# Reordered splits, gathers and routing in a two-stage mixture-of-experts kernel

## The chip, the core and the metric

One core of a Trainium2 chip runs the whole program. The metric is the device time of one execution in microseconds; lower is better. The engines are TensorE (PE, matmul), VectorE (DVE), ScalarE (ACT), GpSimd (POOL) and SyncE (SP), each with its own queue of instructions, which wait on semaphores; DMA queues move data beside them.

## The reference, cut to what matters

The network has four sublayers; attention and a first mixture of experts come before the ones that matter here and are left out below. `x` has 2 x 1024 tokens of 256 numbers.

```python
# _L1_cond: 8 routed experts (top 2) and 2 shared ones, all computed for every token
gp = _leaky(jnp.einsum('th,ehm->etm', x, w_gate))      # hidden width 128
up = jnp.einsum('th,ehm->etm', x, w_up)
y_all = jnp.einsum('etm,emh->eth', gp * up, w_down)
y = (y_sel * topk_w[..., None]).sum(1) + p              # p: the two shared experts
# _L1_ffn, on that y: 8 experts, top 2 by a softmax router
probs = jax.nn.softmax(xf @ w_router, axis=-1)
topk_w, topk_idx = jax.lax.top_k(probs, 2)
h = jax.nn.gelu(jnp.einsum('te,ieh->tih', xf, w1) + b1) # hidden width 1024
out = jnp.einsum('tih,ihe->tie', h, w2) + b2
out = jnp.sum(out * weights[..., None], axis=1)         # weights: zero for experts not chosen
x = x + out
```

## The kernel before

Two stages are touched. All matmuls use float32r in three products: each operand is split into a rounded high part (a copy, mostly on ScalarE) and a low part (a subtraction, on VectorE or POOL), and high x low, low x high and high x high are summed in PSUM.

**The dense stage** (lines 1380 to 1873; 400 to 596 us of the profile from its first steps on) computes `_L1_cond` as 40 steps `s`. A step is one expert and one chunk of 512 tokens. The first eight steps belong to the shared experts. Then the routed experts come, with two chunks each: first for half 0 of the tokens (16 steps, up to `FIRST_HALF` = 24), then for half 1. A group `g` is the steps that share an expert's weights. TensorE runs `up(s + 2)` (L1611, into `pU` and `pG`) and then `down(s)` (L1622, into `pY`). Between them, for one step, ScalarE copies `pG` (L1711), VectorE makes the leaky product (L1786, L1791), ScalarE makes `hidh` (L1731), POOL makes `hidl` (L1551), and VectorE adds `pY` into `xc` (L1851). The expert's next weights are split into `gparts` and `dparts` by ScalarE's `keep_up`, `keep_down` (L1687, L1690) and POOL's `rest_up`, `rest_down` (L1495, L1499), written out in the same per-step loops. `keep_up(g)` waits until `up` of group g - 2 is done. Each engine executes in order, so what is written ahead of `hidh` or `hidl` is in front of them in the queue.

While half 1 is computed, half 0 is routed by pieces of `Slots(0, ...)`, written into the same loops: top 2 (`dve_first`, `dve_second`), `act_exp`, counts, blocks, places, `pool_tokens`, `pe_find`, `dve_tables`. They end in tables `gidx` and `sidx` (tokens of each block of 288). The rows with their probabilities are stored to `ytab` by `sp_rows` (L1284). Near the end, POOL issues `gather(0)`.

**The second phase** (lines 1876 to 2102, from 596 us) computes `_L1_ffn` by blocks of 288 gathered tokens. There are 16 visits `q`, one per half and expert, half 0 first; with these inputs each visit has one block, `j` = `q`. For one block, TensorE does fc1 in 8 chunks `c` of 6 matmuls each (L2001 to L2003, into `pH` with three banks), in the middle `turn_back(j)` (L1975, the block before, transposed into `pX`), after fc1 `turn(j + 1)` (L1364, the next block's rows, into the same `pX`), then fc2 (48 matmuls, L2014 to L2016). ScalarE does 8 gelus (L2042), `gated` in their middle (L2034, scales the turned output by the token's probability `gk` into `yg`), `columns_high` (L1369, `xh`; L1371, `gk`), both high parts of the next expert's weights (L2026, L2027, `keep_high`) and the output's bias (L2055, `yT`). VectorE splits `h` (L2081, L2083), `xl` (L1375) and the weights' low parts (L2068, L2072). POOL's body is `scatter(j)` (L1941, three indirect DMAs that add `yg` to the result) and then `gather(j + 2)` (L1358, three indirect DMAs from `ytab` into `G`). `gather(j + 2)` needs `turn(j + 1)`, which reads the one buffer `G`; `gated(j + 1)` needs `scatter(j)` to have landed, for `yg` is one buffer too. SP loads the weights of split `r`, two DMAs of 1 MB, into a ring of four, as soon as the low parts of split r - 4 are made.

In visits 0 to 5, half 1 is routed by `Slots(1, ...)` on a bank of its own (`pF`). Half 1's rows go to `ytab` from SP's queue, behind the load of r = 3.

## Time and profile before

| | us |
|---|---|
| median of 3 runs | 885.27 |
| lowest, highest | 878.69, 886.39 |
| the profiled execution | 884.36 |
| its span | 882.5 |
| TensorE busy (matmul) | 694.8 (79%) |
| VectorE busy | 474.9 (54%) |
| POOL busy | 395.0 (45%) |
| ScalarE busy | 336.0 (38%) |

The profile is one execution; its span runs from the first to the last recorded instruction. Times in it count from the span's start. A row of the timeline has the start, the duration of all instructions merged in it, the engine, the line of the kernel, the operation with out <- in and the number of instructions, and, in brackets, how long the engine had stood idle in front of it and what released it. "Granted clock" (PEclk) is TensorE's clock as a share of 2.4 GHz; it is granted at two levels, 1.2 and 2.4 GHz, and a share between them is a mean over a stretch. TensorE's matmul records overlap, so its busy time is an upper bound of useful work.

### The profile page before, as it was taken

How to read it: one execution, taken by the hardware profiler on the slowest of the kernel's cores; microseconds unless marked ns; L12 is line 12 of the kernel's file. 1: busy time of each engine (PE TensorE's matmuls, PEld its weight loads, DVE VectorE, ACT ScalarE, POOL GpSimd, SP SyncE). 2: the span in 40 equal slices, each digit the busy share in tenths (PEclk: the TensorE clock that was granted, in tenths of full speed). 3: DMA queues.
4: the chain of work that ended last, by engine and by line, in shares of the span. 5: the costliest groups of instructions: out<-in, count | busy, mean ns of one | idle time of the engine just before them, and what ended most of it. 6: DMA issues, size and time to landing. Idle time of an engine off the chain costs nothing. (4 is left out here: it accounts for less than half of the span.)

```text
span 882.5 us, 14235 instructions
## 1 busy us (share of the span) xinstructions
PE 694.8 (79%) x4385; PEld 636.3 (72%) x4386; DVE 474.9 (54%) x1023; ACT 336.0 (38%) x739; POOL 395.0 (45%) x515
## 2 busy tenths in 40 slices
PE   0777777511699999399989989978888989898991
PEld 0676667501699889387778867768778989898991
DVE  3353554478311111256877788866647855565760
ACT  1243445110133323124233332316746556475660
POOL 2222202000145445423554657636747665755873
PEclk9756675655799999769999999999999989898996
DMA  7870490040089994594000102006496463562222
GB/s 236 136 182 14 108 325 0 6 117 4 13 273 320 299 308 121 161 321 148 25 24 25 36 25 74 1 15 212 129 354 148 119 188 82 138 206 46 42 45 31
DMA packets 91760, 111.56 MB, mean 126 GB/s; under 512 B 9632, under 2 KB 80672, under 8 KB 91296
## 3 DMA queue, kind: packets, MB, share of 16 engines
q1 hardware_dynamic: 75072, 90.74, 33.4%
q0 software_dynamic: 11536, 14.30, 9.5%
q10 hardware_dynamic: 5072, 5.52, 1.9%
q8 instruction: 42, 0.69, 0.3%
q14 instruction: 38, 0.31, 0.1%
HBM read 93.84 MB, written 17.32 MB: 126 GB/s over the span
## 5 line engine op out<-in xcount | busy, mean ns | idle before, releaser
L1941 POOL DMA_INDIRECT out<-nyg,si x51 | 88.6, 1737 | 20.5 <-issue 20.2
L121 POOL TENSOR_TENSOR held<-ones 128x1 f32<-128x1 f32 x137 | 45.8, 334 | 116.2 <-ACT nyg L2034 53.8
L2042 ACT ACTIVATE nh<-npH,c_sb 128x288 f32<-128x288 f32 x128 | 62.1, 502 | 39.1 <-PE npH L2003 36.9
L1358 POOL DMA_INDIRECT nG<-ytab,gi x54 | 63.9, 1184 | 14.6 <-issue 13.0
L2081 DVE CAST nhh<-nh 128x576 fp32r<-128x576 f32 x64 | 33.0, 516 | 66.6 <-ACT nh L2042 66.6
L1851 DVE SCALAR_TENSOR_TENSOR xc<-pY,W,xc 128x264 f32<-128x264 f32 x160 | 67.3, 483 | 2.7 <-PE pY L1622 2.7
L1551 POOL TENSOR_TENSOR hidl<-sums,hidh 128x512 fp32r<-128x512 f32 x40 | 56.1, 1403 | 23.5 <-ACT hidh L1731 23.5
L1611 PE MATMUL pU<-xparts,gparts 128*128 128x512 f32 x240 | 65.5, 409 | 1.1 <-DVE xparts L1782 1.1
L1611 PE MATMUL pG<-xparts,gparts 128*128 128x512 f32 x240 | 64.1, 403 | 2.5 <-ACT sums L1711 2.5
L1786 DVE SCALAR_TENSOR_TENSOR sums<-sums 128x512 f32<-128x512 f32 x40 | 40.9, 1023 | 42.2 <-ACT sums L1711 41.7
L1104 PEld LDWEIGHTS mpH<-mXT,w_sb 128*128 128x128 f32 x512 | 61.2, 196 | 1.8 <-DVE mXT L1135 1.1
L1104 PE MATMUL mpH<-mXT,w_sb 128*128 128x128 f32 x512 | 61.5, 280 | 0.7 <-DVE mXT L1135 0.7
L1622 PE MATMUL pY<-dparts,hidh 128*128 128x264 f32 x320 | 60.7, 284 | 0.0
L1622 PE MATMUL pY<-dparts,hidl 128*128 128x264 f32 x160 | 47.7, 298 | 14.8 <-POOL hidl L1551 8.2
L1123 ACT ACTIVATE mhT<-mpH,b_sb 128x128 f32<-128x128 f32 x128 | 36.1, 371 | 59.6 <-PE mpH L1104 59.6
L1112 PE MATMUL mpY<-w_sb,mhT 128*128 128x256 f32 x256 | 58.2, 380 | 0.0
L1611 PEld LDWEIGHTS pG<-xparts,gparts 128*128 128x128 f32 x240 | 46.3, 194 | 14.3 <-ACT sums L1711 3.2
L1112 PEld LDWEIGHTS mpY<-w_sb,mhT 128*128 128x128 f32 x256 | 47.4, 190 | 6.0
L1611 PEld LDWEIGHTS pU<-xparts,gparts 128*128 128x128 f32 x240 | 44.0, 195 | 9.4 <-DVE xparts L1782 1.5
L1622 PEld LDWEIGHTS pY<-dparts,hidh 128*128 128x128 f32 x320 | 49.7, 188 | 0.8
L2083 DVE TENSOR_TENSOR nhl<-nh,nhh 128x576 fp32r<-128x576 f32 x64 | 48.6, 759 | 2.2
L1495 POOL TENSOR_TENSOR gparts<-gw,gparts 128x512 fp32r<-128x512 f32 x18 | 23.4, 1298 | 58.8 <-ACT gparts L1687 48.1
(412 smaller groups left out, 1891.8 us busy)
## 6 DMA issues: line engine op xcount, KB each, us to landing
w_sb<-in_w SPq DMA_DIRECT2D x32, 1024.0 KB, 8.3
w_sb<-in_v SPq DMA_DIRECT2D x30, 1024.0 KB, 9.8
bias_sb<-in_bias SPq DMA_DIRECT2D x4, 1024.0 KB, 14.2
gw<-in_wgate SPq DMA_DIRECT2D x17, 128.0 KB, 2.2
gw<-in_wup SPq DMA_DIRECT2D x17, 128.0 KB, 2.3
ytab<-xc SPq DMA_DIRECT2D x2, 1056.0 KB, 5.1
acc<-zrow SPq DMA_DIRECT2D x1, 2056.0 KB, 24.6
sums<-acc SPq DMA_DIRECT2D x4, 514.0 KB, 6.0
```

The costliest lines, as they stand in the source:

```text
L121: pool.tensor_tensor(held[:, n:n + 1], ones[:, 0:1], ones[:, 0:1], ALU.mult)
L1104: ins = pe.matmul(pH[:, c // 4, (c % 4) * P:(c % 4 + 1) * P], w1_sb[:, u, k, c * P:(c + 1) * P], XT[:, k], start=(k == 0), stop=(k == KD - 1))
L1112: ins = pe.matmul(pY[:, 0:D], hT[:, c], w2_sb[:, u, c], start=(c == 0), stop=(c == FC - 1))
L1358: pool.indirect_dma_start(G[:, n], None, ytab, bass.IndirectOffsetOnAxis(ap=gi3[:, n:n + 1], axis=0)).then_inc(gathered, 16)
L1551: pool.tensor_tensor(hidl[:, s % 2], hid[:, s % 2], hidh[:, s % 2], ALU.subtract).then_inc(lo_ready, 1)
L1611: ins = pe.matmul(pp, gparts[:, g % 2, wn, cs], xparts[:, xn, k, chunk], start=(k == 0 and (wn, xn) == (0, 1)), stop=(k == KD - 1 and (wn, ...
L1622: ins = pe.matmul(pY[:, j, 0:YROW], hn[:, s % 2, j * P:(j + 1) * P], dparts[:, e, wn], start=(hn is hidl), stop=(hn is hidh and wn == 0))
L1786: dve.scalar_tensor_tensor(lk, ga, 0.01, ga, ALU.mult, ALU.max).then_inc(lk_ready, 1)
L1851: dve.scalar_tensor_tensor(xc[:, t], pY[:, j, 0:YROW], W[:, t, e:e + 1], xc[:, t], ALU.mult, ALU.add).then_inc(acc_done, 1)
L1941: pool.indirect_dma_start(result, bass.IndirectOffsetOnAxis(ap=si3[:, n:n + 1], axis=0), yg[:, n], None, bounds_check=B * N - 1, oob_is_er ...
L2042: act.activation(h[:, c], pH[:, c % HBANKS, 0:WIDE], ACT.Gelu_apprx_tanh, bias=c1_sb[:, e, c:c + 1]).then_inc(gelu_done, 1)
L2083: dve.tensor_tensor(hl[:, two], h[:, two], hh[:, two], ALU.subtract).then_inc(h_ready, 1)
```

## The change

- Dense stage: ScalarE and POOL make `hidh` and `hidl` at the start of their part of a step, and the splits, constants and token products stand behind them. `keep_up` and `rest_up` of group g are placed in step first_of[g] - 3 instead of first_of[g] - 4. The last routing pieces of half 0 come one step earlier, and `gather(0)` is placed in the last step, behind its `hidl`, instead of the last but one.
- Second phase: POOL gathers first and scatters second. `turn_back` gets two banks `pZ` of its own, stands behind fc1 next to `turn`, and `gated` stands behind `columns_high` and the first weight split. `pH` has two banks instead of three, and half 1's routing pieces use a part of `pZ`. `gk` has four slots instead of two.
- Half 1's routing: the matmul pieces follow the first chunk of fc1 in visits 1, 2, 3 and 6, and TensorE waits ahead of `turn_back` until they are read. VectorE's pieces stand at a visit's start. `pool_tokens` go to visits 4 and 5, ahead of the gather. The exponential and the counts stand ahead of visit 1's gelus. ScalarE stores half 1's rows in visit 2.

```diff
@@ -1197 @@
-        gk = sb("gk", [SUB, 2 * NSUB, E1], into=late)
+        gk = sb("gk", [SUB, 4 * NSUB, E1], into=late)
@@ -1216 @@
-        M_SET, LESS, PROBS, BLOCKS = range(1, 5)
+        M_SET, LESS, PROBS, BLOCKS, READ = range(1, 6)
@@ -1235, class Slots @@
                 self.pC = bank[0:TE, TE:TE + P]
-                self.pT = bank[0:E1, TE + P:TE + 2 * P]
-                self.pN = bank[0:1, TE + 2 * P:TE + 2 * P + E1]
-                self.pM = bank[0:SUB, TE + 2 * P + E1:TE + 2 * P + E1 + self.cols]
+                self.pT = bank[0:E1, TE:TE + P]
+                self.pM = bank[0:SUB, TE:TE + self.cols]
+                self.pN = bank[0:1, TE + P:TE + P + E1]
...
-            def sp_rows(self, sp):
+            def rows_out(self, eng):
...
-                link(dve.tensor_copy(nblk[:, self.hf], self.pN))
+                dve.tensor_copy(nblk[:, self.hf], self.pN).then_inc(r_dve, 1)
@@ -1532, dense stage, POOL @@
                     for s in range(LAST + 1):
                         e, c = STEPS[s]
+                        pool.wait_ge(hi_ready, s + 1)
+                        if s >= 2:
+                            pool.wait_ge(down_done, 4 * s - 4)
+                        pool.tensor_tensor(hidl[:, s % 2], hid[:, s % 2], hidh[:, s % 2], ALU.subtract).then_inc(lo_ready, 1)
                         if s == 1:
                             rest_up(1)
                         for g in range(2, len(GROUPS)):
-                            if first_of[g] - 4 == s:
+                            if first_of[g] - 3 == s:
                                 rest_up(g)
...
+                        if s == FIRST_HALF + 8:
+                            slots.pool_tokens(pool, 0)
                         if s == FIRST_HALF + 9:
-                            slots.pool_tokens(pool, 0)
-                        if s == FIRST_HALF + 10:
                             slots.pool_tokens(pool, 1)
-                        pool.wait_ge(hi_ready, s + 1)
-                        if s >= 2:
-                            pool.wait_ge(down_done, 4 * s - 4)
-                        pool.tensor_tensor(hidl[:, s % 2], hid[:, s % 2], hidh[:, s % 2], ALU.subtract).then_inc(lo_ready, 1)
...
-                        if s == LAST - 1:
+                        if s == LAST:
                             pool.wait_ge(tables, 1)
                             pool.wait_ge(y_out, 16)
                             gather(pool, 0, 0)
@@ -1668, dense stage, TensorE @@
-                        if s == FIRST_HALF + 11:
+                        if s == FIRST_HALF + 10:
                             slots.pe_find(pe)
@@ -1720, dense stage, ScalarE @@
-                        for g in range(2, len(GROUPS)):
-                            if first_of[g] - 4 == s:
-                                keep_up(g)
-                        if s == 2 or 6 <= s < FIRST_HALF - 2 and s % 2 == 0:
-                            keep_down(1 if s == 2 else GROUPS[group_at[s + 2]])
                         act.wait_ge(hid_ready, s + 1)
                         if s >= 2:
                             act.wait_ge(down_done, 4 * s - 4)
                         act.activation(hidh[:, s % 2], hid[:, s % 2], ACT.Copy).then_inc(hi_ready, 1)
+                        for g in range(2, len(GROUPS)):
+                            if first_of[g] - 3 == s:
+                                keep_up(g)
+                        if s == 2 or 6 <= s < FIRST_HALF - 2 and s % 2 == 0:
+                            keep_down(1 if s == 2 else GROUPS[group_at[s + 2]])
@@ -1866, dense stage, VectorE @@
-                        if part == 12:
+                        if part == 11:
                             slots.dve_tables(dve, slot_link)
@@ -1885, second phase @@
-            pH = ps("npH", [P, 3, 512], ph)
+            pZ = ps("npZ", [P, 2, 512], ph)
+            pH = ps("npH", [P, 2, 512], ph)
             pY = ps("npY", [P, 2, 512], ph)
-            pF = ps("npF", [P, 512], ph)
-            slots = Slots(1, pF, A1, hot1, tok1s)
-            HBANKS = 3
+            slots = Slots(1, pZ[:, 1, D:2 * D], A1, hot1, tok1s)
+            HBANKS = 2
@@ -1923, SP @@
-                        if r == RING - 1:
-                            slots.sp_rows(sp)
@@ -1948, POOL @@
+                        if first and q in (4, 5):
+                            slots.pool_tokens(pool, q - 4)
...
-                        scatter(j, hf)
                         pool.wait_ge(turned, j + 2)
                         pool.wait_ge(gk_ready, j + 2)
                         pool.wait_ge(gathered, j * (16 * NSUB) + 32 * NSUB)
                         held_here(pool, 1)
                         gather(pool, j + 2, hf)
-                        if first and q == 4:
-                            for n in range(2):
-                                slots.pool_tokens(pool, n)
+                        scatter(j, hf)
@@ -1969, TensorE @@
-                                ins = pe.transpose(pX[0:SUB, n // 2, (n % 2) * D + k * P:(n % 2) * D + (k + 1) * P],
+                                ins = pe.transpose(pZ[0:SUB, n // 2, (n % 2) * D + k * P:(n % 2) * D + (k + 1) * P],
...
+                        if first and q in (1, 2, 3, 6):
+                            pe.wait_ge(yg_ready, j)
                         for c in range(FC):
-                            if c == FC // 2:
-                                turn_back(j)
-                                if first and q == 1:
-                                    slots.pe_count(pe)
...
                             ins.then_inc(fc1_done, 1)
-                        pe.wait_ge(yg_ready, j + 1)
+                            if first and c == 0:
+                                if q == 1:
+                                    slots.pe_count(pe)
...
+                                if q == 6:
+                                    slots.pe_find(pe)
+                        if first and q == 1:
+                            pe.wait_ge(r_act, 2 + COPIED)
+                        if first and q in (2, 3):
+                            pe.wait_ge(r_dve, 5 + (BLOCKS if q == 2 else READ))
+                        if first and q == 6:
+                            pe.wait_ge(tables, 2)
+                        turn_back(j)
                         turn(pe, pX, j + 1)
@@ -2024, ScalarE @@
-                    def keep_high(r):
+                    def first_high(r):
                         act.wait_ge(w_in[r % RING], 32 * (W_ROUND + 1 + r // RING))
                         act.activation(w1h[r % 2], raw1[r % RING], ACT.Copy).then_inc(w_hi, 1)
+
+                    def second_high(r):
                         act.activation(w2h[r % 2], raw2[r % RING], ACT.Copy).then_inc(w_hi, 1)
                     def gated(j, e):
-                        slot = (j + 1) % 2
+                        slot = (j + 3) % 4
...
+                        if first and q == 1:
+                            slots.act_exp(act)
+                            slots.act_counts(act)
                         for c in range(FC):
                             act.wait_ge(fc1_done, j * FC + c + 1)
                             act.activation(h[:, c], pH[:, c % HBANKS, 0:WIDE], ACT.Gelu_apprx_tanh,
                                            bias=c1_sb[:, e, c:c + 1]).then_inc(gelu_done, 1)
-                            if c == FC // 2:
-                                gated(j, VISITS[max(q - 1, 0)][1] if first else e)
                         columns_high(act, pX, j + 1)
-                        if first and q == 1:
-                            slots.act_exp(act)
-                            slots.act_counts(act)
-                        if first and q + 1 < 2 * E1 and split_of[q + 1] != split_of[q]:
+                        split = first and q + 1 < 2 * E1 and split_of[q + 1] != split_of[q]
+                        if split:
                             act.wait_ge(fc2_done, j + 1)
-                            keep_high(split_of[q + 1])
+                            first_high(split_of[q + 1])
+                        gated(j, VISITS[max(q - 1, 0)][1] if first else e)
+                        if split:
+                            second_high(split_of[q + 1])
+                        if first and q == 2:
+                            slots.rows_out(act)
@@ -2075, VectorE @@
                     def body(j, q, first):
+                        if first and q == 0:
+                            slots.dve_second(dve, slot_link)
+                        if first and q == 1:
+                            slots.dve_probs(dve, slot_link)
+                        if first and q == 2:
+                            slots.dve_blocks(dve, slot_link)
+                        if first and q == 3:
+                            slots.dve_places(dve, slot_link)
+                        if first and q == 6:
+                            slots.dve_tables(dve, slot_link)
                         for p in range(FC // 2):
...
-                        if first and q == 5:
-                            slots.dve_tables(dve, slot_link)
```

## Rows read from the trace of the kernel before

**Rows 1.** Busy time by stretch: a quiet block, then one with a stall; start:end, length, engines, PEclk.

```profile
724.00:738.00 14.00, 14.00 (x111) 13.99 (x110) 5.57 (x9) 6.40 (x15) 6.00 (x9) 1.00 0.66 180
...
752.00:772.00 20.00, 17.03 (x112) 16.79 (x111) 11.02 (x12) 10.06 (x17) 15.38 (x20) 0.83 0.60 152
```

**Rows 2.** TensorE's waits from 596 us on: us in total, times, longest.

```profile
PE npX L1364 <- DMA nG<-ytab,gi: 18.9, 6, 5.0
```

**Rows 3.** TensorE's waits from 400 to 596 us, same columns.

```profile
PE pY L1622 <- POOL hidl L1551: 8.2, 10, 2.9
```

**Rows 4.** Timeline, TensorE: starts of four `up` steps; start, duration, then [idle before <- releaser].

```profile
427.31 1.55 PE L1611 MATMUL pU<-xparts,gparts 128*128 128x512 f32 x6
...
503.55 0.63 PE L1611 MATMUL pU<-xparts,gparts 128*128 128x512 f32 x2
...
507.79 1.55 PE L1611 MATMUL pU<-xparts,gparts 128*128 128x512 f32 x6
...
581.50 1.56 PE L1611 MATMUL pU<-xparts,gparts 128*128 128x512 f32 x6
```

**Rows 5.** Timeline, ScalarE, one of the dense stage's splits (`keep_up`).

```profile
465.70 0.63 ACT L1687 ACTIVATE gparts<-gw 128x512 fp32r<-128x512 f32 x1 [4.03 <-PE pG L1611]
```

**Rows 6.** Timeline: ScalarE releases TensorE, in the routing part of the dense stage.

```profile
526.22 0.58 ACT L1711 ACTIVATE sums<-pG 128x512 f32<-128x512 f32 x1
...
526.86 1.42 PE L1611 MATMUL pG<-xparts,gparts 128*128 128x512 f32 x5 [2.48 <-ACT sums L1711]
```

**Rows 7.** Timeline, end of the dense stage and start of the second phase.

```profile
585.38 0.58 POOL L1354 COPY gi<-gidx 96x3 uint32<-96x3 uint32 x1 [1.05 <-DVE sidx L1350]
...
586.67 0.63 ACT L1731 ACTIVATE hidh<-sums 128x512 fp32r<-128x512 f32 x1 [1.58 <-DVE sums L1791]
...
590.48 1.31 POOL L1551 TENSOR_TENSOR hidl<-sums,hidh 128x512 fp32r<-128x512 f32 x1
...
594.79 0.76 DVE L1375 TENSOR_TENSOR nxl<-pU,nxh 128x576 fp32r<-128x576 f32 x1 [0.58 <-ACT nxh L1369]
...
597.65 0.60 PE L2001 MATMUL npH<-nxh,w1l 128*128 128x288 f32 x1 [3.58 <-issue]
```

**Rows 8.** Timeline, ScalarE, a quiet block: gelus, then a weight split.

```profile
835.22 1.01 ACT L2042 ACTIVATE nh<-npH,c_sb 128x288 f32<-128x288 f32 x2 [0.19 <-issue]
836.52 0.50 ACT L2042 ACTIVATE nh<-npH,c_sb 128x288 f32<-128x288 f32 x1 [0.29 <-PE npH L2003]
...
842.30 1.90 ACT L2026 ACTIVATE w1h<-w_sb 128x2048 fp32r<-128x2048 f32 x1
```

**Rows 9.** Timeline: gather, scatter, a stalled turn, and the next gather beside VectorE's splits.

```profile
755.99 1.14 POOL L1358 DMA_INDIRECT nG<-ytab,gi  x1 [0.30 <-issue]
...
758.47 0.19 POOL L121 TENSOR_TENSOR held<-ones 128x1 f32<-128x1 f32 x1 [1.00 <-ACT nyg L2034]
...
762.12 1.22 PE L1364 MATMUL npX<-ident,nG 96*128 96x96 f32 x6 [2.97 <-DMA nG<-ytab,gi]
...
762.97 1.43 POOL L1941 DMA_INDIRECT out<-nyg,si  x1 [0.30 <-issue]
...
765.97 2.29 DVE L2068 TENSOR_TENSOR xparts<-w_sb,xparts 128x2048 fp32r<-128x2048 f32 x1 [1.15 <-ACT xparts L2026]
...
769.37 1.87 POOL L1358 DMA_INDIRECT nG<-ytab,gi  x1 [0.30 <-issue]
```

**Rows 10.** Timeline, ScalarE: one of two table loads around half 1's exponential.

```profile
622.79 1.28 ACT L1269 ACT_TABLE_LOAD   x1
```

**Rows 11.** Timeline, the kernel's tail.

```profile
862.58 0.89 ACT L2055 ACTIVATE nyT<-npY,c_sb 128x288 f32<-128x288 f32 x2 [5.64 <-PE npY L2016]
864.72 1.19 ACT L2034 ACTIVATE nyg<-npX,gk 96x256 f32<-96x256 f32 x3 [1.25 <-PE npX L1975]
...
873.67 0.19 POOL L121 TENSOR_TENSOR held<-ones 128x1 f32<-128x1 f32 x1 [1.95 <-DMA out<-nyg,si]
```

**Rows 12.** DMA issues from 596 us on: last number is median us from issue to landing.

```profile
out<-nyg,si POOLq DMA_INDIRECT x51, 3.6
```

More of the change, by code:

```diff
@@ L1279, in dve_probs @@
                 dve.tensor_tensor(router_rows(self.hf), hexp[:], bcast(hred[:, 3], E1), ALU.mult).then_inc(r_dve, 1)
-            def sp_rows(self, sp):
-                sp.wait_ge(r_dve, 4 * self.hf + PROBS)
+            def rows_out(self, eng):
+                eng.wait_ge(r_dve, 5 * self.hf + PROBS)
                 rows = slice(self.hf * HT * P, (self.hf + 1) * HT * P)
-                sp.dma_start(ytab[rows, :].rearrange("(t p) d -> p t d", p=P),
+                eng.dma_start(ytab[rows, :].rearrange("(t p) d -> p t d", p=P),
                              xc[:, self.hf * HT:(self.hf + 1) * HT]).then_inc(y_out, 16)
@@ L1369, in columns_high @@
             act.activation(xh[:], pX[:, :, 0:WIDE], ACT.Copy).then_inc(xh_ready, 1)
-            slot = ds((j % 2) * NSUB, NSUB) if not isinstance(j, int) else slice((j % 2) * NSUB, (j % 2 + 1) * NSUB)
+            slot = ds((j % 4) * NSUB, NSUB) if not isinstance(j, int) else slice((j % 4) * NSUB, (j % 4 + 1) * NSUB)
             act.activation(gk[:, slot], G[:, :, D:YROW], ACT.Copy).then_inc(gk_ready, 1)
@@ L1986, in body @@
                         pe.wait_ge(x_ready, j + 1)
+                        if first and q in (1, 2, 3, 6):
+                            pe.wait_ge(yg_ready, j)
                         for c in range(FC):
-                            if c == FC // 2:
-                                turn_back(j)
-                                if first and q == 1:
-                                    slots.pe_count(pe)
-                                if first and q == 2:
-                                    slots.pe_totals(pe)
-                                if first and q == 3:
-                                    slots.pe_places(pe)
-                                if first and q == 5:
-                                    slots.pe_find(pe)
                             pe.wait_ge(gelu_done, j * FC + c + 1 + FC - HBANKS if c >= HBANKS else j * FC + FC)
@@ L2087, in body @@
                             low_second(split_of[q + 1])
-                        if first and q == 0:
-                            slots.dve_second(dve, slot_link)
-                        if first and q == 1:
-                            slots.dve_probs(dve, slot_link)
-                        if first and q == 2:
-                            slots.dve_blocks(dve, slot_link)
                         if first and q == 3:
-                            slots.dve_places(dve, slot_link)
                             slots.dve_hot(dve, 0)
@@ L2098, in body @@
                             slots.dve_hot(dve, 1)
-                        if first and q == 5:
-                            slots.dve_tables(dve, slot_link)
                     per_block(dve, "dve", body)
```

16 lines of the change are left out of this document (10 added, 6 removed).

## The prediction

> **What bounds the kernel now.** I read the busy table of single stretches first, then TensorE's waits, then the timeline at the places that these name. TensorE sets the pace of both stages that the diff touches. In a quiet block of the second phase it is busy for the whole 14.0 us at full clock; in another block of the same work the stretch is 20 us long, TensorE is busy for 17.0 of it, and the granted clock is 0.83 [rows 1]. The difference is the turn of the next block's rows, which waits for gathered data: 18.9 us in 6 waits, the longest 5.0 [rows 2]. A stall costs more than its length. A wait of 2.97 [rows 9] makes that block 6.0 longer, because the matmuls behind it run at 1.2 GHz for a while. The sixteen blocks take 264.9 us, from the first matmul at 597.65 [rows 7] to the end of the last fc2 at 862.5 [rows 11], where sixteen quiet ones would take 224.
>
> In the dense stage, TensorE waits 8.2 us in 10 waits for `hidl` on POOL [rows 3]. A free step is 4.24 us long (503.55 to 507.79). The 17 steps from 427.31 to 507.79 take 80.5 instead of 72.1, so 8.4 are lost; the 14 from 507.79 to 581.50 take 73.7 instead of 59.4, so 14.3 are lost [rows 4]. In the first of these stretches the reader sees why: ScalarE stands idle 4.03 us in front of `keep_up`, waiting for TensorE's later `up` [rows 5], and `hidh` of the step, ready long before, is queued behind it; `hidl` comes later still.
>
> The sum is made against the profiled execution: 884.4 us with a span of 882.5. The median of the three runs is 885.3, 0.9 above it.
>
> **Part 1, dense order.** `hidh` and `hidl` now go first, and the splits follow one step later (first_of - 3), by when the `up` that they wait for is done: the 4.03 wait vanishes. The split is still due only when TensorE reaches that group, about two steps (8.5 us) after it can start, which covers one ScalarE and one POOL instruction of 0.6 and 1.3 us (`hidl` has 1.31 in [rows 7]). POOL's constants and token products also go behind `hidl`. Of the 8.4 I take 7. Of the 14.3, VectorE's routing chain is the cause of at least the 2.48 wait [rows 6] and routing matmuls are real work; neither goes away, and I take 5. Sum: 12 us gained. Bounds: 4, if little more than the listed waits other than the last goes, and 16.
>
> **Part 2, first gather.** `gather(0)` moves behind the last `hidl`. Before, it starts at 585.38 and holds that `hidl` until 590.48 [rows 7], which is the longest wait of [rows 3] (2.9). In the new order the last `hidl` can start when its `hidh` ends, 587.3, and end at 588.6; the gather follows. With 5.1 for its copy and its issues, the third of these starts about 1.5 before their end, at 592.2; landing takes between 3.6 [rows 12] and 6.1 (755.99 to the turn at 762.12 [rows 9]). Turn, `xh` and `xl` add 2.2, so x is ready at 598.0 to 600.5, where it was 595.55 [rows 7]. I take the quiet landing, since no weight load runs there: 2.5 us lost (bounds 2.5 and 5). The routing pieces of half 0 move one step forward, so the tables are not late.
>
> **Part 3, gather ahead of scatter.** Times here count from the end of a turn. In the block behind the stall at 762.12 (the turn ends at 763.34) the gather waited for nothing but this turn: its third issue ended at 771.24, 7.9 after it, with VectorE's weight splits alongside [rows 9]. In the new order every gather runs like this one. Its third issue starts at 6.0 and lands between 9.6 and 12.1; the next turn starts at about 13.5. So the data come 1.4 to 3.9 early and the six stalls go. A second cause goes with them: the router rows left SP's queue, where they held back the loads of r = 4 to 6 until half 1's probabilities were ready. Now ScalarE issues that store, one instruction, in a place with idle time. In exchange the loads of r = 2, 3 and 4 all start with the phase, and `gather(1)` lands among them. I put 1 us on this.
>
> **Part 4, two banks instead of three for fc1.** In a quiet block ScalarE makes a gelu in 0.50 and idles 0.29 per chunk [rows 8]. With two banks this 0.29 is the whole slack for the handoff and for TensorE's drain. A matmul starts 0.06 after the ScalarE instruction that releases it (526.80 to 526.86 [rows 6]), so the steady chunks just fit. The first chunk of a block does not: its gelu starts at 835.22, after the bias of the block before and a gap of 0.19 [rows 8], about 0.3 later than the data. I take 0.4 per block, 6.4 in all (bounds 0 and 12). TensorE's turn into banks of its own is as long as before, and only moves.
>
> **Part 5, half 1's routing.** At q = 1 the exponential and the counts now stand ahead of the first gelu: two table loads of 1.28 [rows 10] and two short copies, 3.1 us, of which 0.3 is hidden: 2.8, and 1.2 for a fall of the clock that may follow (0 to 3.0, the price in [rows 1] and [rows 9]). The counting, totals, places and find matmuls stay the same work, 4.9.
>
> **Part 6, the scatter's buffer and the tail.** Behind a gather come the scatters. From 757.13 to 764.40 they took 7.3, of which 1.0 was a wait for ScalarE [rows 9]; so the third now starts at 7.9 + 4.85 = 12.75, POOL is free at 14.2, and at 3.6 [rows 12] it lands at 16.4. Next block's `gated`, which overwrites `yg`, wants this landing at its own turn + 2.6, that is 14.4 + 2.6 = 17.0, and ScalarE has 0.5 to spare behind it (one split is 1.90 [rows 8]). It fits by about 1 us; under a weight load, with 6.1, it doesn't. I put 2 us on it. At the end nothing covers it. Before, the last `gated` starts at 864.72 and the scatter behind it has landed at 873.67 [rows 11]. Now it waits for the preceding scatter to land. Without splits beside its gather (2.3 less) that is 16.4 - 2.3 = 14.1 after the turn, or, with 6.3 for fc2, 7.8 after the last fc2, where `gated` started 2.2 after it. The tail grows by 5.6 us.
>
> **The sum.** Second phase: 224 + 6.4 + 2.5 (cold start, as now) + 4.0 + 4.9 = 241.8 against 264.9, 23.1 gained. In all: -12 + 2.5 - 23.1 + 1 + 2 + 5.6 = -24.0, so 884.4 - 24 = 860.
>
> **A rule against it.** SBUF — State Buffer (the Trainium skill), section "SBUF: two separate sides", says that some VectorE instructions hold the port pair that POOL shares for their whole length, and that POOL writes no descriptors meanwhile. Parts of the trace agree: an issue beside the splits took 1.87, where one of another gather without them took 1.14 [rows 9]. By the rule a gather that meets two splits would be stopped for all of both.
>
> **The rivals.** *POOL is held for both splits in full:* one split is 2.29 [rows 9], two are 4.6, and the 7.9 holds about half of that already. POOL would then be free at 16.5 instead of 14.2. The next gather can begin 0.8 after its turn, so a block would last 15.7 instead of 14.4; thirteen blocks with splits make 860 + 17 = 877. Against it: the 7.9 was measured beside two splits. Chance 0.08.
> *The dense gain turns into waits for VectorE*, which has its own chain there [rows 6]: 3 instead of 12, 869. Chance 0.10.
> *The gathers still come late*, the change not doing what it says: landing would have to take over 7.5. At three of six stalls with 6.0 each: 878. The longest landing in [rows 9] is 6.1, against it. Chance 0.06.
> *Slower than before:* POOL becomes the bound. The place is POOL's queue, gather and then scatter in each block, with `gated` behind the landing. It decides against the kernel when a block takes 16.7 instead of 14.4, that is from a POOL free at 17.5, 3.3 later than the rows give; fifteen blocks then cost 34.5, 894.5. Against it stands that all the pieces are measured; for it, that the slack is only 1 us and that the splits, scatter and loads meet in a new order. Chance 0.07.
> *Better:* two banks cost nothing, the dense stage gains 16, and the clock holds: 860 - 6.4 - 4 - 1.2 = 848. Chance 0.14.
>
> **The numbers.** The forecast has 0.52, with a range of its own of 852 to 868; the remaining 0.03 lies between the cases. About 1% (8.9 us) is what a measurement of this kernel tells from no change, so faster means below 876.4. The forecast, the better case, the dense rival and some of the remainder give 0.81; the two cases at 877 and 878 fall within 1% and give, with a little of the remainder, 0.12; slower is 0.07. The range of 846 to 877 takes in the forecast, the dense rival and most of the better case, and leaves out about 0.2.
>
> **What would show it.** In the changed kernel's waits, TensorE's turn should have at most one wait for `nG`, and blocks of the second phase should be 14.3 to 14.7 apart at granted clock 1.0. ScalarE's `keep_up` should lose its wait for TensorE, and the dense steps should be 4.24 to 4.3 outside the routing chain. The last `gated` should start about 7.8 after the last fc2. A wait of TensorE for gelu in every chunk would show part 4 wrong; POOL busy from turn to turn without a pause, or `gated` waiting for a scatter, part 6. The forecast is wrong most easily in part 6, where 1 us of slack per block decides.

## The result, and the profile after

The kernel after takes 856.1 us (median; 855.4 to 857.8) where the kernel before takes 882.0 on the same chips: 0.970 of it, with an interval of 0.966 to 0.974. Forecast were 860.0, in a range of 846 to 877. The profiled execution has a span of 853.6 against 882.5.

That span is 28.9 shorter, but not all of it is the change's. I cut both spans at three points: the start of the dense stage's fourth `up` step, which comes 13.6 us behind the third (router matmuls stand between them); the first fc1 matmul; the last bias of fc2. What follows the last bias is the tail. A block is counted from bias to bias.

| us | ahead of the dense steps | dense steps to first fc1 | sixteen blocks | tail | span |
|---|---|---|---|---|---|
| before | 406.1 | 191.6 | 264.9 | 19.9 | 882.5 |
| after | 401.8 | 182.6 | 244.0 | 25.2 | 853.6 |
| difference | -4.3 | -9.0 | -20.9 | +5.3 | -28.9 |

The first column is code that the change leaves alone, but for the first three dense steps. In the fourteen profiles of this case it ends anywhere from 397.2 to 411.7 (402.8 in d2 below, which has the dense stage of before), so its -4.3 is not counted as the change's. The change itself is worth the other three, -24.6; the medians say -25.9.

The blocks, as busy time by stretch of the kernel after (start:end, length, then TensorE, weight loads, VectorE, ScalarE, GpSimd, granted clock, DMA share, GB/s): the first block, half 1's exponential (q = 1), two blocks beside weight splits with a quiet one between:

```profile
584.35:601.11 16.76, 16.72 (x108) 16.43 (x108) 10.56 (x20) 9.65 (x17) 6.11 (x8) 0.84 1.04 364
601.11:618.36 17.25, 15.18 (x112) 14.57 (x113) 10.87 (x15) 13.22 (x21) 11.46 (x13) 1.00 0.56 173
650.07:665.95 15.88, 14.64 (x110) 14.04 (x108) 13.66 (x13) 10.12 (x19) 13.36 (x13) 1.00 0.61 175
712.02:726.23 14.21, 14.21 (x110) 14.00 (x109) 8.85 (x11) 10.35 (x18) 8.64 (x9) 1.00 0.24 35
755.96:771.79 15.83, 15.60 (x118) 15.08 (x116) 10.12 (x11) 10.28 (x19) 13.32 (x16) 1.00 0.60 177
```

Against [rows 1] none of the sixteen blocks is 20 us long and only the first has a granted clock under 1.0. Quiet blocks are those without weight splits or routing. TensorE's waits from 400 us on (total, times, longest):

```profile
PE npH L1990 <- ACT nh L2051: 5.6, 6, 1.6
...
PE pU L1364 <- DMA nG<-ytab,gi: 4.0, 1, 4.0
...
PE pY L1622 <- POOL hidl L1538: 0.2, 1, 0.2
```

The six waits for `nG` of [rows 2] are gone; one is left, at the first turn. `hidl` fell from 8.2 [rows 3] to 0.2. New are six waits for a gelu. The dense stage in the timeline: the three `up` steps that answer to the first, third and fourth of [rows 4], and one `keep_up` for [rows 5]:

```profile
422.99 1.32 PE L1611 MATMUL pU<-xparts,gparts 128*128 128x512 f32 x5
...
496.27 1.55 PE L1611 MATMUL pU<-xparts,gparts 128*128 128x512 f32 x6
...
566.62 1.56 PE L1611 MATMUL pU<-xparts,gparts 128*128 128x512 f32 x6
...
459.95 0.62 ACT L1687 ACTIVATE gparts<-gw 128x512 fp32r<-128x512 f32 x1
```

Seventeen steps now take 73.3 (80.5), the next fourteen 70.4 (73.7), and `keep_up` waits for nothing. The end of the stage, for [rows 7]:

```profile
572.38 1.29 POOL L1538 TENSOR_TENSOR hidl<-sums,hidh 128x512 fp32r<-128x512 f32 x1 [2.85 <-ACT hidh L1726]
573.61 0.18 POOL L1354 COPY gi<-gidx 96x3 uint32<-96x3 uint32 x1
...
579.57 1.19 PE L1364 MATMUL pU<-ident,nG 96*128 96x96 f32 x6 [4.04 <-DMA nG<-ytab,gi]
581.48 0.76 DVE L1375 TENSOR_TENSOR nxl<-pU,nxh 128x576 fp32r<-128x576 f32 x1 [5.04 <-ACT nxh L1369]
584.35 0.60 PE L1990 MATMUL npH<-nxh,w1l 128*128 128x288 f32 x1 [3.58 <-issue]
```

From the last `up` to the first fc1 it is 17.73, where it was 16.15. The end of one of the long blocks, ScalarE's waits for a scatter from 584 to 830 us, and the landing of the scatters (issue lines, last number), for [rows 12]:

```profile
768.90 1.19 ACT L2040 ACTIVATE nyg<-npZ,gk 96x256 f32<-96x256 f32 x3 [2.56 <-DMA out<-nyg,si]
769.98 1.91 ACT L2033 ACTIVATE w2h<-w_sb 128x2048 fp32r<-128x2048 f32 x1
771.79 0.88 ACT L2065 ACTIVATE nyT<-npY,c_sb 128x288 f32<-128x288 f32 x2
...
773.11 0.40 PE L1990 MATMUL npH<-nxh,xparts 128*128 128x288 f32 x1 [1.39 <-ACT nh L2051]
...
ACT nyg L2040 <- DMA out<-nyg,si: 20.9, 11, 3.4
...
out<-nyg,si POOLq DMA_INDIRECT x51, 5.0
```

The gates (`gated`) wait 2.56 for the scatter; behind them stand the second weight split and the bias; the gelus are late and TensorE stops 1.39. The median landing went from 3.6 to 5.0, and this is a mixture. Blocks 0 to 11, in which weights are loaded, and the rest, in which none are:

```profile
out<-nyg,si POOLq DMA_INDIRECT x33, 5.9
...
out<-nyg,si POOLq DMA_INDIRECT x18, 3.4
```

In before the same two are 3.8 and 3.5. The tail, for [rows 11]:

```profile
828.39 0.89 ACT L2065 ACTIVATE nyT<-npY,c_sb 128x288 f32<-128x288 f32 x2 [1.02 <-PE npY L2020]
835.99 1.19 ACT L2040 ACTIVATE nyg<-npZ,gk 96x256 f32<-96x256 f32 x3 [6.71 <-DMA out<-nyg,si]
...
844.79 0.19 POOL L121 TENSOR_TENSOR held<-ones 128x1 f32<-128x1 f32 x1 [1.89 <-DMA out<-nyg,si]
```

### The profile page after: what moved, and what is told of

It reads as the page before. It is cut to its first block and busy times, and to the rows that moved or that the text cites. A ratio compares the mean times of both kernels' runs of the same rounds, so it can differ in the third digit from the quotient of the medians.

```text
span 853.6 us, 14267 instructions
## 1 busy us (share of the span) xinstructions
PE 681.3 (80%) x4385; PEld 624.7 (73%) x4386; DVE 477.6 (56%) x1023; ACT 341.7 (40%) x739; POOL 401.6 (47%) x515
## 5 line engine op out<-in xcount | busy, mean ns | idle before, releaser
L1939 POOL DMA_INDIRECT out<-nyg,si x51 | 82.2, 1611 | 17.9 <-issue 17.9
L1538 POOL TENSOR_TENSOR hidl<-sums,hidh 128x512 fp32r<-128x512 f32 x40 | 52.2, 1305 | 76.4 <-ACT hidh L1726 76.4
L1358 POOL DMA_INDIRECT nG<-ytab,gi x54 | 77.4, 1434 | 16.3 <-issue 16.2
L1726 ACT ACTIVATE hidh<-sums 128x512 fp32r<-128x512 f32 x40 | 25.3, 631 | 80.3 <-DVE sums L1791 80.3
L1786 DVE SCALAR_TENSOR_TENSOR sums<-sums 128x512 f32<-128x512 f32 x40 | 38.8, 970 | 28.7 <-ACT sums L1711 28.1
L2103 DVE TENSOR_TENSOR nhl<-nh,nhh 128x576 fp32r<-128x576 f32 x64 | 50.9, 796 | 2.2
L2101 DVE CAST nhh<-nh 128x576 fp32r<-128x576 f32 x64 | 31.8, 497 | 30.9 <-ACT nh L2051 30.6
```

Source lines behind the costliest of these rows:

```text
L1358: pool.indirect_dma_start(G[:, n], None, ytab, bass.IndirectOffsetOnAxis(ap=gi3[:, n:n + 1], axis=0)).then_inc(gathered, 16)
L1538: pool.tensor_tensor(hidl[:, s % 2], hid[:, s % 2], hidh[:, s % 2], ALU.subtract).then_inc(lo_ready, 1)
L1786: dve.scalar_tensor_tensor(lk, ga, 0.01, ga, ALU.mult, ALU.max).then_inc(lk_ready, 1)
L1939: pool.indirect_dma_start(result, bass.IndirectOffsetOnAxis(ap=si3[:, n:n + 1], axis=0), yg[:, n], None, bounds_check=B * N - 1, oob_is_er ...
L2103: dve.tensor_tensor(hl[:, two], h[:, two], hh[:, two], ALU.subtract).then_inc(h_ready, 1)
```

## Experiments

The columns are those of the table above, from each kernel's profiled execution; the ratio is to the kernel before, timed beside it.

| kernel | median us | ratio, interval | dense to fc1 | blocks | tail |
|---|---|---|---|---|---|
| d1, dense part alone | 872.7 | 0.992 [0.988, 0.995] | 182.1 | 260.3 | 19.9 |
| d2, second phase alone | 867.9 | 0.986 [0.980, 0.992] | 194.0 | 244.3 | 25.2 |
| d3, order without late splits | 858.6 | 0.976 [0.969, 0.982] | 187.5 | 243.8 | 25.3 |
| d4, late splits without order | 858.1 | 0.979 [0.969, 0.989] | 185.5 | 243.7 | 25.2 |
| p1, scatter first | 913.0 | 1.035 [1.029, 1.040] | 181.8 | 303.7 | 20.9 |
| c1, gather first, old banks | 937.8 | 1.064 [1.058, 1.069] | 182.3 | 324.6 | 24.0 |
| p2, two `yg` | 855.7 | 0.970 [0.965, 0.975] | 182.6 | 248.4 | 24.6 |
| p6, second split ahead of gates | 855.5 | 0.970 [0.965, 0.975] | 182.1 | 244.9 | 25.2 |
| p4, first gather early | 855.1 | 0.969 [0.964, 0.975] | 179.6 | 243.7 | 25.2 |
| b1, five edits | 861.7 | 0.976 [0.970, 0.982] | 183.8 | 245.4 | 24.7 |
| b2, b1 with another tail | 859.4 | 0.976 [0.970, 0.981] | 182.9 | 247.9 | 23.8 |
| b3, tokens on VectorE | 850.3 | 0.966 [0.962, 0.971] | 182.7 | 241.2 | 21.3 |

### The two parts, each alone (d1, d2)

d1 takes only the dense hunks into the kernel before, d2 takes them out of the kernel after. In d1, for instance:

```diff
-                            if first_of[g] - 4 == s:
+                            if first_of[g] - 3 == s:
...
-                        if s == LAST - 1:
+                        if s == LAST:
```

> The kernel before with the change's dense hunks alone (hidden block's high and low parts ahead of the weight splits, splits three steps ahead, half 0's tokens and tables one step earlier, first gather behind the last low part); second phase as before. Theory (the two parts add up): the dense part ends 14.9 us earlier and the first turn loses 1.6 us of it, as the two traces put up(39) and the first fc1 matmul, so about 13.3 us under the kernel before: 867 to 870 where before is 882. Rival (the gain of the dense part depends on the second phase, or the second phase's late gathers swallow it): 875 to 882.

> The kernel after with its dense hunks undone (dense part as before, second phase as after). Theory: the sixteen blocks keep their 20.9 us and the tail its loss of 5.2 us, so about 15.7 us under the kernel before: 865 to 868 where before is 882. Rival (the second phase gains because the dense part left something ready for it): 872 to 880.

d2 came as expected. d1 fell between the two cases, and the expectation was at fault: its 14.9 compared two clock times, and 4.3 of them belong to the stage ahead. By its own stage d1 gains 9.5, about what after does (9.0). Its ten executions lie between 863.0 and 875.5, and the profiled one is the fastest; those of after lie within 2.4. By medians d1 gains 7.9 and d2 12.8, and these fall 5 short of the 25.9 of both. Of this, 2.4 is visible: d2, which has the dense stage of before, takes 194.0 there instead of 191.6, with a granted clock of 0.76 from the last `up` to the first fc1, where before has 1.00. The rest is not explained. What d1 also gives is a bound for the price of two banks: it has three, and its quiet blocks, in the same view as above, are 13.9 long, against 14.2 in after. Of the 0.3, fc1 has 0.2 and the moved `turn_back` 0.1; no run changes the banks alone.

```profile
784.99:798.89 13.90, 13.90 (x110) 13.89 (x109) 9.39 (x11) 10.12 (x18) 6.70 (x7) 1.00 0.18 25
```

### Order or lateness of the splits (d3, d4)

d3 sets the distance back to four steps; d4 moves the high and low parts back behind the splits.

```diff
-                            if first_of[g] - 3 == s:
+                            if first_of[g] - 4 == s:
```

> The kernel after, with the splits of the next expert's weights back at four steps ahead; the hidden block's high and low parts stay ahead of them. Theory (what cost the dense part was the split's WAIT standing ahead of the high part, so that order alone gives most): at most 3 us over the kernel after, 856 to 859. Rival (the wait costs wherever it stands, since the next step's high part is behind it): 8 us or more over it, 864 to 868.

> The kernel after, with the high and low parts of the hidden block back behind the weight splits; the splits stay three steps ahead, where their wait for TensorE's previous use of the buffer is over. Theory (the wait was the cost, so its lateness alone gives most too): at most 4 us over the kernel after, 856 to 860. Rival (the splits' own time ahead of the high and low part is the cost, some 1 us on ScalarE and 2 to 4 us on GpSimd in every second step): 8 us or more over it, 864 to 870.

Both medians are where the theory put them, 2.5 and 2.0 over after, too near each other to rank (d4's four executions are 856.3 to 859.0 and one of 869.1). The stage itself tells more. From the fourth to the last `up` it takes 175.4 before, 170.3 in d3, 168.1 in d4 and 164.8 in after. The starts of the `up` steps that answer to the first, third and fourth of [rows 4], d3 and then d4:

```profile
423.69 1.55 PE L1611 MATMUL pU<-xparts,gparts 128*128 128x512 f32 x6
...
497.49 1.56 PE L1611 MATMUL pU<-xparts,gparts 128*128 128x512 f32 x6
...
571.22 1.56 PE L1611 MATMUL pU<-xparts,gparts 128*128 128x512 f32 x6
```
```profile
422.17 1.55 PE L1611 MATMUL pU<-xparts,gparts 128*128 128x512 f32 x6
...
495.05 1.55 PE L1611 MATMUL pU<-xparts,gparts 128*128 128x512 f32 x6
...
569.10 1.56 PE L1611 MATMUL pU<-xparts,gparts 128*128 128x512 f32 x6
```

The seventeen steps take 73.8 and 72.9 (before 80.5, after 73.3): there either half of the edit is enough by itself. In d3 `keep_up` still waits, some 1.2 at a time, and does no harm behind `hidh`; in d4 it does not wait, and the splits' own time ahead of `hidl` costs nothing. So what cost these steps was the wait standing ahead of `hidh`. One `keep_up` of d3:

```profile
458.06 0.63 ACT L1687 ACTIVATE gparts<-gw 128x512 fp32r<-128x512 f32 x1 [1.23 <-PE pG L1611]
```

The fourteen steps with the routing take 73.7 and 74.1, as before (73.7), and 70.4 in after: there neither half alone gains anything. In d4 two waits for `hidl` make 4.6; the longer one stands behind a token product, for which GpSimd had waited 7.11 ahead of `hidl`:

```profile
541.64 2.16 POOL L1328 TENSOR_TENSOR w_sb<-w_sb,token 128x432 f32<-128x432 f32 x1 [7.11 <-DVE w_sb L1321]
...
545.07 0.59 PE L1622 MATMUL pY<-dparts,hidl 128*128 128x264 f32 x1 [3.54 <-POOL hidl L1551]
```

In d3 the loss is spread over several waits, with a granted clock of 0.98, and its cause stays open.

### Gather first, and the banks that it needs (p1, c1)

p1 turns the two calls in GpSimd's body round again. c1 is d1 with the same two calls in the new order, and nothing else of the second phase.

```diff
-                        scatter(j, hf)
                         pool.wait_ge(turned, j + 2)
...
                         gather(pool, j + 2, hf)
+                        scatter(j, hf)
```

> The kernel after with GpSimd's body turned round again: scatter of the block before first, then the gather; banks, four gate slots and everything else as after. Theory (part 3: the order is what ended the six stalls): gates at 2.1 us after a quiet turn, scatter issues to 7.6, gather issues to 11.8, landing 2.8: data at 14.6 after a turn, for a next turn due at 13.4, so 1 us late in quiet blocks and 3 to 5 in those with weight splits: 20 to 45 us over the kernel after, 876 to 900, with waits for the gathered rows in most blocks. Rival (the gathers have slack in either order; the gain came from the turns' own banks): within 4 us of the kernel after, 854 to 860.

> The kernel before with the dense part of after and one more line: GpSimd issues the gather before the scatter; three banks for fc1, the turn and the turn back in one bank pair, gates in the middle of fc1 as before. Theory (gathering first needs the turns' own banks: the gates wait for the scatter, which lands some 15 us after a turn's end, and the next turn waits for the gates, which were due 3 us ahead of it): no wait for gathered rows, but a wait for the gates of 2 to 5 us at nearly every turn, 890 to 915, slower than the 873 of the dense part alone. Rival (the order alone ends the six stalls and the banks are not needed): 854 to 862.

TensorE's waits, p1 and then c1:

```profile
PE npX L1364 <- DMA nG<-ytab,gi: 44.1, 13, 4.9
```
```profile
PE npX L1364 <- ACT nyg L2034: 49.0, 12, 7.0
```

Both went the theory's way and further: the expectations left out the clock behind each wait (granted clocks down to 0.83 over a block of p1 and 0.77 in c1), and c1 waits another 7.4, once, for half 1's token product. p1 shows that in the new arrangement the order ends the late gathers. It has the router rows off SP's queue as after has, so that alone does not end them. c1 shows that in the old arrangement the order only trades them for the gates, which must empty the bank that the turn wants and wait for the scatter now standing behind the gather. Either half alone is slower than before.

### The long blocks (p2, p6)

p2 gives the gates two buffers in turn; p6 moves one line, shown here.

```diff
                             first_high(split_of[q + 1])
+                            second_high(split_of[q + 1])
                         gated(j, VISITS[max(q - 1, 0)][1] if first else e)
-                        if split:
-                            second_high(split_of[q + 1])
```

> The kernel after with two buffers for the gated rows, so that the gates of a block no longer wait for the landing of the scatter just issued (they wait for the one before). Theory (the blocks of 15.2 to 16.2 us under weight splits are long because the gates wait for the scatter, the second weight split, the bias and the first gelu stand behind them): blocks 2 to 4, 10 and 11 come to about 14.6, 5 to 6 us in all, 850 to 852. Rival (they are long because VectorE's low parts of the weights stand ahead of the hidden low parts): no change, 855 to 857.

> The kernel after with one line moved: in a block with a weight split ScalarE makes the high part of the second matrix right behind that of the first, and the gates come behind both. Theory (as for the two buffers: the second split is late because the gates wait for the scatter): 3 to 6 us under the kernel after, 850 to 853, and the gates 1.9 us later at no cost. Rival (the gates' lateness then delays the bias and the scatter as much): 855 to 858.

The totals did not move, so as a forecast both fell. The blocks did: 2, 4 and 11, which were 15.6, 15.9 and 15.8 long, became 14.8, 14.3, 14.5 in p2 and 14.6, 14.2, 14.5 in p6. The gain went elsewhere: in both at block 5, from 14.4 to 20.4 and 21.0, and in p2 at block 3 as well, from 16.2 to 18.5, behind a wait of 1.27 ahead of the routing matmuls (granted clock 0.91). Block 5 in p2's timeline:

```profile
657.57 3.04 DVE L2078 TENSOR_TENSOR xparts<-w_sb,xparts 128x2048 fp32r<-128x2048 f32 x1 [1.15 <-ACT xparts L2030]
657.91 2.73 POOL L121 TENSOR_TENSOR held<-ones 128x1 f32<-128x1 f32 x1
658.04 4.79 POOL L1354 COPY gi<-gidx 96x3 uint32 x1
660.53 2.28 DVE L2082 TENSOR_TENSOR w2l<-w_sb,w2h 128x2048 fp32r<-128x2048 f32 x1
...
673.07 0.71 PE L1364 MATMUL npX<-ident,nG 96*128 96x96 f32 x6 [4.45 <-DMA nG<-ytab,gi]
```

With the second split no longer held up, VectorE runs both without a gap, and half 1's tokens (2.01) had kept GpSimd back until then. Its two short instructions, `held` of 128x1 and the list copy of 96x3, take 0.19 and 0.18 where nothing stands beside them. Here the first ends with the first split and the copy with the second, and TensorE waited 4.45 for the gather behind them. In after the same two splits stood 2.1 us apart and GpSimd's list had been copied ahead of both (the first starts at 661.72):

```profile
659.17 0.18 POOL L1354 COPY gi<-gidx 96x3 uint32 x1
```

A missing gap alone is not the cause. In before and in p6 VectorE runs all fourteen pairs of splits without one, and GpSimd loses a whole pair at one place in each: where the list copy meets it. A gather whose list is copied already gets its issues in, each some 1.3 longer. The trace of before has both cases:

```profile
626.38 4.49 POOL L1354 COPY gi<-gidx 96x3 uint32 x1
...
766.80 2.27 POOL L1358 DMA_INDIRECT nG<-ytab,gi  x1 [0.30 <-issue]
```

The clock added to the price. In p6 the corresponding wait is 3.83, and block 5 is 6.6 longer than in after; over the ten microseconds behind the wait the granted clock was 0.69.

```profile
672.50:682.40 9.90, 9.90 (x56) 9.90 (x57) 5.27 (x3) 5.48 (x8) 9.05 (x8) 0.69 0.20 25
```

### The first gather (p4)

```diff
-                        if s == LAST:
+                        if s == LAST - 1:
                             pool.wait_ge(tables, 1)
```

> The kernel after with the first gather one step earlier, where before had it (behind the low part of the last step but one, ahead of that of the last). Theory (part 2: its issues hold GpSimd for 3.5 us, which the low part of the last step must wait for): the last step's down matmuls wait 2 to 4 us, the first turn does not wait; the first fc1 comes within 1 us of that of after, 855 to 858. Rival (there is room for it): 2.5 to 4 us under the kernel after, 852 to 854.

The end of the dense stage in p4's timeline:

```profile
572.65 1.30 POOL L1538 TENSOR_TENSOR hidl<-sums,hidh 128x512 fp32r<-128x512 f32 x1
...
574.00 0.39 PE L1622 MATMUL pY<-dparts,hidl 128*128 128x264 f32 x1 [1.66 <-POOL hidl L1538]
...
579.81 0.60 PE L1990 MATMUL npH<-nxh,w1l 128*128 128x288 f32 x1 [3.58 <-issue]
```

The trace sides with the rival: TensorE waits only 1.66 for the last low part, and the first fc1 comes 14.8 after the last `up`. It takes 17.2 to 17.8 in after, d1, d3, d4, p1, p2 and p6, which all have the late gather, so by the traces the change's move of this gather costs 2.4 to 3.0. The median is 1.0 under after's, with executions from 850.5 to 857.3, and cannot settle it.

### Together (b1, b2, b3)

b1 takes p2, p6 and p4, puts the tokens between gather and scatter, and moves the exponential (and, not shown, the counts):

```diff
-                        if first and q == 1:
-                            slots.act_exp(act)
-                            slots.act_counts(act)
...
+                        if first and q == 0:
+                            slots.act_exp(act)
                         columns_high(act, pX, j + 1)
```

b2 adds, in the last visit, the scatter ahead of the gather. b3 is b1 with the tokens' product on VectorE and no gather in the last visit's first block:

```diff
                             slots.dve_hot(dve, 1)
+                            slots.pool_tokens(dve, 1)
...
+                        if not (last and first):
```

> The kernel after with five edits: two buffers for the gated rows; the high part of the second matrix ahead of the gates; half 1's tokens between the gather and the scatter, so that the list of the next gather is copied before VectorE's two weight splits; the first gather one step earlier; half 1's exponential at the end of block 0 and its counts behind the first gelu of block 1. Theory (the two-buffer kernel gave its gain back at one turn, where GpSimd's copy of 96x3 stood 4.8 us beside two weight splits): no wait for gathered rows at a turn, block 5 at 14.3 to 14.8 instead of 20.4, block 1 at 14.5 to 15 instead of 17.25, blocks 2, 4, 11 at 14.3 to 14.8: about 6 us from the blocks, 2 to 3 from the exponential and 0 to 5 from the first gather: 843 to 850. Rival (GpSimd is held wherever its copy stands, and another turn is late): 852 to 857.

> The kernel with the five edits and, in the last visit alone, the scatter ahead of the gather (whose rows no block uses). Theory (the tail pays for three gather issues of 1.3 us each ahead of the last scatter but one): 3 to 4 us under the kernel with the five edits. Rival (the last scatter but one waits for the landing of the scatter before it, not for the issues): 0 to 1 us under it.

> The kernel with the five edits, with half 1's tokens multiplied on VectorE behind its one-hot pieces instead of on GpSimd, and without the last visit's first gather, whose rows no block uses. Theory (that kernel's block 6 is 25 us long because the tokens wait on GpSimd behind a gather whose list was copied beside two weight splits, TensorE waits 5.5 us for them and its clock falls): block 6 comes back to 16.9, the find's own length, 8 us under the kernel with the five edits, and the tail 1 us: 850 to 853 median, 3 to 6 us under the kernel after. Rival (VectorE's extra 1 us in blocks 4 and 5 makes the hidden low parts late): blocks 4 and 5 at 15 or more, 855 or more.

b1 missed by 12. Blocks 1, 2, 4, 5 and 11, which the expectation named, are 14.2 to 14.6, as expected or shorter; block 6 is 25.2: GpSimd again copied a list beside two splits (4.79), the tokens stood behind that gather, and `find` waited. In b1's timeline and by stretch:

```profile
687.57 0.78 PE L1335 MATMUL npZ<-hot,A 128*96 128x99 f32 x3 [5.54 <-POOL hot L1328]
```
```profile
687.60:697.00 9.40, 9.40 (x62) 9.33 (x63) 3.44 (x10) 2.01 (x4) 4.65 (x5) 0.72 0.58 122
```

In b2 the tail fell by 0.9, as its rival said: its gather merely moved in front of the last scatter. b3's median came out as forecast, its parts only in part. Block 6 is 8.3 shorter than in b1 (8 forecast). The tail is 3.4 shorter, where 1 was put, and that covers two losses: block 3 is 18.0, as in b2 (0.7 us of waiting ahead of the routing matmuls, granted clock 0.9), and block 5 is 15.9, over the mark that the rival set, though by a wait of 1.47 for gathered rows and not by the low parts. By stretch, its block with the counts (17.25 in after) and its block with `find`:

```profile
605.37:619.53 14.16, 14.16 (x108) 13.74 (x108) 10.45 (x15) 10.38 (x19) 10.80 (x13) 1.00 0.55 172
...
682.22:699.09 16.87, 16.87 (x142) 16.80 (x141) 11.43 (x18) 10.33 (x17) 10.53 (x13) 1.00 0.56 159
```

The tail is 21.3 instead of 25.2. b3's six executions (846.6 to 852.8) all lie under after's four, its median 5.8 under; the two ratios' intervals still overlap. It still waits 3.3 for the last `hidl`, where p4 waits 1.7: three more start-up DMAs for its second buffer stand there on GpSimd, 0.62 each.

## Why the prediction was right, and where it was not

The forecast counted -24.0 and the stages moved -24.6. By the columns of the table it had put -9.5, -20.1 and +5.6, and -9.0, -20.9 and +5.3 came. So the total stands for the reasons given, stage by stage; inside the stages there are errors that nearly cancel, and that they do is luck.

- **Part 1, dense order.** 12 forecast, 10.6 measured between the fourth and the last `up`. The first stretch gave 7.2 (7), and d3 and d4 bear out its mechanism, the wait ahead of `hidh`. The second gave 3.4 (5), and only with both halves of the edit. TensorE's waits for VectorE's `xc` from 400 us on are 3.7 in all, where before had 5.8, so the rival of that name did not happen.
- **Part 2, first gather.** 2.5 lost forecast, 1.6 between the profiles of before and after. This 1.6 is not shown to be the change's: d2, with the code of before, takes 17.9 from the last `up` to the first fc1, at the lower clock. The rows landed 2.8 after the start of the third issue rather than 3.6. What the part did not ask is whether the move was needed: p4 says it was not once `hidl` goes first.
- **Part 3.** All six stalls went, as derived; p1 brings them back as thirteen. The 1 us for loads that start together was not tried and stays open.
- **Part 4, two banks.** 0.4 per block forecast against 14.0; quiet blocks are 14.2, 0.2 over that and 0.3 over d1's 13.9. No wait for a gelu in every chunk. That the turns needed banks of their own, which the part took for granted, is c1's result.
- **Part 5.** Right in kind, too dear by the clock: block 1 is 3.05 over a quiet one, forecast 2.8 plus 1.2, and the clock held at 1.0. b1 to b3 place the exponential at the end of block 0 and remove 1.5 to 2.2 of it: blocks 0 and 1 together go from 34.0 to 31.8, 32.4 and 32.5.
- **Part 6.** The term that was mis-sized. The mechanism is the one named, and its sizes came: a scatter lands in 3.4 where no weights are loaded (3.6 put) and in 5.9 in the blocks with loads (6.1 put). What was too small is the 2 us put on it. Eleven times before the tail the gates wait for a scatter, the sign that the prediction gave for this part being wrong, and where the second split and the bias stand behind them, TensorE stops: blocks 2, 3, 4, 10 and 11 lose 4.5 in all against p6. The tail was 5.6 forecast and 5.3 measured, with the last gates 7.6 after the last bias starts (7.8).
- **The rule held against it.** "SBUF — State Buffer" (the Trainium skill), section "SBUF: two separate sides", has GpSimd stopped while VectorE holds the shared port. Where GpSimd's two short instructions met a pair of splits without a gap (before, d1, p2, p6, b1, b2), the traces agree: one ended with each split, and the copy of 0.18 took 4.5 to 4.8. Elsewhere it cost about 1.3 for one issue, and GpSimd got the next in between. In after the rival priced by it did not occur; the long blocks, which its 15.7 would also fit, come to 14.2 to 14.8 in p6 with GpSimd's order unchanged (block 3 apart). I dismissed it because measured issues already held half of the price. [rows 9] show only the cheap place: the 4.49 at 626.38 stood in the same trace, ahead of the longest stall of [rows 2] (5.04 in the timeline).
- **The rivals.** Late gathers, POOL as the bound and the better case did not come; 856 is inside the forecast's own range of 852 to 868. Against late gathers stood a longest landing of 6.1, from [rows 9] alone. Ahead of that longest stall the third issue starts at 633.82 and the turn at 641.98, so a landing of 8.2, over the 7.5 that this rival needs, was on the trace. The shares of the outcomes do not add up as said either: forecast, better case, dense rival and the whole remainder make 0.79 and not 0.81, the two cases at 877 and 878 make 0.14 and not 0.12.

## What to carry to other kernels

Putting the producer of the next block's data first on a queue pays only if whatever then stands second has no reader in the next block's way: here the order needed banks of its own, and without them it was 6% slower than before. When one delay is taken away, look at what it kept apart, and at which instruction of the other engine now stands there: here a copy of 0.18 cost a whole pair of splits, and an issue at the same place 1.3. Compare stages between marks of their own, since clock times carry along whatever ran differently ahead of them.

## What the runs showed of the hardware

- GpSimd instructions of 128x1 and 96x3 take 0.19 and 0.18 us. Started beside two VectorE subtractions of 128x2048 (2.3 each, once 3.0) without a gap between them, the first took 2.4 to 2.7 and ended with the first subtraction, the second took 4.5 to 4.8 and ended with the second, in all six traces that have the case.
- A gather's issue takes 0.9 to 1.1 alone, 2.2 to 2.3 across two such subtractions (p6) and up to 2.6 beside one (after); a scatter's takes 1.4 to 1.7, and up to 3.6 beside one (after).
- A wait of 3.83 us at a turn in p6 left the granted clock at 0.69 over the next 9.9 us, a mixture of the 2.4 and 1.2 GHz levels: the block grew by 6.6, not by 3.8. Waits of 0.7 to 1.3 in block 3 of p2, b2 and b3 came with 0.90 to 0.91 over the block; waits of 1.1 to 1.6 for a gelu in after left it at 1.0.
- The median landing of the scatters was 3.5 us before and 3.4 after in blocks without weight loads, 3.8 and 5.9 in blocks with them; why the loads cost more in after was not tried.
- The same code ahead of the dense steps, but for the first three, ended between 397.2 and 411.7 us.
